# One change to an attention and feed-forward kernel: the score maxima from half of TensorE's rows, two query tiles at a time

## The reference

```python
y = x * jax.lax.rsqrt(jnp.mean(x * x, axis=-1, keepdims=True) + RMS_EPS) * rms_w
y = jnp.einsum('bsm,cm->bsc', y, w_in)
...
q = _rope(q)
k = _rope(k)
qk = jnp.einsum('bghsd,bgxpd->bghsp', q, k) * DQK ** (-0.5)
causal = jnp.tril(jnp.ones((s, s), dtype=bool))
qk = jnp.where(causal, qk, -jnp.inf)
attn = jax.nn.softmax(qk, axis=-1)
o = jnp.einsum('bghsp,bgxpd->bghsd', attn, v)
```

## Time and profile before

| | |
|---|---|
| median of the runs shown | 1998.78 us (1995.89 to 2000.47) |
| the profiled execution's own time | 2001.82 us |
| its span, first to last instruction | 2000.0 us |
| PE busy in the span | 1920.8 us (96%) |
| POOL busy in the span | 1423.1 us (71%) |
| attention stage, first to last of POOL's low parts | 71 to 1462 us |
| mean granted clock of TensorE | 0.983 of full speed |

### The profile page before, as it was taken

The page is one execution under the profiler, slowest core; times in us unless marked ns, Lnnn a source line. Parts: engine busy times, 40 slices in busy tenths (PEclk is TensorE's granted clock), DMA queues, the critical chain, the costliest instruction groups (busy, mean ns, idle before and its releaser), DMA issues. The chain is left out here.

```text
span 2000.0 us, 55133 instructions
## 1 busy us (share of the span) xinstructions
PE 1920.8 (96%) x21382; PEld 1184.5 (59%) x21382; DVE 1233.8 (62%) x3283; ACT 936.9 (47%) x1969; POOL 1423.1 (71%) x1627
## 2 busy tenths in 40 slices
PE   4999979999999999999999999999969998999999
PEld 3566656666666666666666666666634443444444
DVE  7787568668768776876887687687625562221221
ACT  4465546556655565665556566555622211111110
POOL 1799979999999999999999999999920001121211
PEclk7999989999999999999999999999989999999999
DMA  6342262244225224321522442152156520000000
GB/s 209 67 78 39 67 147 49 44 65 74 46 41 105 49 44 70 73 45 39 105 49 44 76 70 48 33 94 47 37 183 217 209 85 1 16 5 21 5 16 22
DMA packets 301572, 136.79 MB, mean 68 GB/s; under 512 B 248336, under 2 KB 285456, under 8 KB 299792
## 3 DMA queue, kind: packets, MB, share of 16 engines
q1 hardware_dynamic: 301328, 133.43, 29.6%
HBM read 49.48 MB, written 25.17 MB: 37 GB/s over the span
## 5 line engine op out<-in xcount | busy, mean ns | idle before, releaser
L786 POOL TENSOR_TENSOR pl<-p 128x512 f16<-128x512 f32 (+3 forms) x1280 | 1137.4, 919 | 38.6 <-ACT p L635 35.3
L635 ACT ACTIVATE p<-a_ps 128x512 f32<-128x512 f32 (+3 forms) x1280 | 677.5, 532 | 570.9 <-PE a_ps L568 333.9
L701 DVE TENSOR_REDUCE mpart<-a_ps 128x1 f32<-128x512 f32 x768 | 508.6, 685 | 140.6 <-PE a_ps L552 136.0
L584 PE MATMUL a_ps<-v,p 128*128 128x65 f16 x4352 | 528.1, 193 | 6.2 <-POOL pl L786 5.6
L586 PE MATMUL a_ps<-v,p 128*128 128x64 f16 x4352 | 530.6, 194 | 0.0
L588 PE MATMUL a_ps<-v,pl 128*128 128x65 f16 x4352 | 527.4, 192 | 0.0
L584 PEld LDWEIGHTS a_ps<-v,p 128*128 128x128 bf16 x4352 | 412.7, 97 | 110.1 <-issue 7.9
L586 PEld LDWEIGHTS a_ps<-v,p 128*128 128x128 bf16 x4352 | 406.1, 97 | 108.3 <-issue 0.3
L552 PE MATMUL a_ps<-k_hl,q_hh 128*128 128x512 f16 (+3 forms) x1280 | 429.7, 348 | 17.0 <-issue 15.7
L568 PE MATMUL a_ps<-q_lm,k_h 128*128 128x512 f16 (+3 forms) x1280 | 444.6, 347 | 0.0
L567 PE MATMUL a_ps<-q_hh,k_hl 128*128 128x512 f16 (+3 forms) x1280 | 443.7, 347 | 0.0
(11 more groups left out here) (95 smaller groups left out, 2268.6 us busy)
## 6 DMA issues: line engine op xcount, KB each, us to landing
attn_scratch<-o_turn SPq DMA_DIRECT2D x64, 256.0 KB, 3.0
p_att<-attn_scratch SPq DMA_DIRECT2D x32, 512.0 KB, 4.3
raw<-ffn_t SPq DMA_DIRECT2D x12, 1024.0 KB, 5.0
wraw<-w_in_t SPq DMA_DIRECT2D x8, 768.0 KB, 5.3
resid_scratch<-raw SPq DMA_DIRECT2D x4, 1024.0 KB, 4.4
raw<-w_out_t SPq DMA_DIRECT2D x1, 4096.0 KB, 15.9
x<-resid_scratch SPq DMA_DIRECT2D x4, 1024.0 KB, 8.0
out<-x SPq DMA_DIRECT2D x16, 256.0 KB, 2.1
```

Source lines behind the costliest of these rows:

```text
L584: nc.tensor.matmul(o, weights, v[:, par, j, 0:VU], start=(j == 0 and t == 0), stop=False, skip_group_check=True)
L635: nc.scalar.activation(p32[:, i % RING, r * P:CHUNK], sbank(i)[:, r * P:CHUNK], ACT.Exp, scale=SCALE).then_inc(exp_done, 1)
L701: nc.vector.reduce_max(mpart[:, u % 2, t, kk:kk + 1], bank, AX.X).then_inc(maxs_used, 1)
L786: nc.gpsimd.tensor_tensor(pl[:, i % RING, cols], p32[:, i % RING, cols], p_high[:, i % RING, cols], ALU.subtract).then_inc(low_ready, 1)
```

## The change

The product for the maxima uses k's high part alone, which is 64 rows deep. Two of them run as a pair: the first takes rows 0 to 63 of `q_hh` and of `k_h1`, the second rows 64 to 127 of `q_hh` and of `k_hl`, which both hold the high parts. The pair is two query tiles against the same chunk of keys, each into its own bank; both banks are taken before the first product. `query_and_key_tile` puts the pieces in an order in which two that follow each other are such a pair. The order of the slots moves each second piece into the slot of the first. Nothing else is changed: the number and the widths of the products and of DVE's reductions are the same.

```diff
@@ -249,7 +249,7 @@
 def opening():
 
     out = [(None, ("proj", 0, t), []) for t in range(2 * TPC)] + [(None, None, [])] * 2
-    out += [(None, None, [(0, u, i)]) for u in range(HG) for i in range(KEY_TILES[u])]
+    out += [(None, None, [(0, u, i), (0, u, i + 1)]) for u in range(HG) for i in range(0, KEY_TILES[u], 2)]
     return out
...
         for i in range(KEY_TILES[u]):
-            pieces[begin + i * (end - begin) // KEY_TILES[u]].append((ahead, u, i))
+            pieces[begin + i // 2 * 2 * (end - begin) // KEY_TILES[u]].append((ahead, u, i))
...
-            for item in [("piece", *p) for p in pieces[:1]] + ([job] if job else []) + [("piece", *p) for p in pieces[1:]]]
+            for item in [("piece", *p) for p in pieces[:2]] + ([job] if job else []) + [("piece", *p) for p in pieces[2:]]]
+
+
+def query_and_key_tile(u, i):
+
+    pair, second = divmod(i, 2)
+    both, kk = divmod(pair, u // HG + 1)
+    return 2 * both + second, kk
...
-                def max_piece(ahead, u, i):
+                def max_pair(ahead, u, i):
                     c, h = divmod(u, HG)
-                    t, kk = divmod(i, c + 1)
                     if i == 0:
                         pe.wait_ge(hh_in[c % 2][h], 16 * (2 * (g + ahead) + c // 2 + 1))
                         if h == 0:
                             pe.wait_ge(k_in[c], 32 * (g + ahead + 1))
-                    bank = take_bank("piece", ahead, u, i)
-                    width = CHUNK if kk < c else (t + 1) * P
-                    nc.tensor.matmul(bank[:, 0:width], q_hh[:, c % 2, h, t * P:(t + 1) * P],
-                                     k_hl[:, par ^ ahead, kk * CHUNK:kk * CHUNK + width], start=True, stop=True)\
-                        .then_inc(maxs_ready, 1)
+                    banks = [take_bank("piece", ahead, u, n) for n in (i, i + 1)]
+                    for n, (rows, keys) in enumerate(((slice(0, DH), k_h1), (slice(DH, P), k_hl))):
+                        t, kk = query_and_key_tile(u, i + n)
+                        width = CHUNK if kk < c else (t + 1) * P
+                        nc.tensor.matmul(banks[n][:, 0:width], q_hh[rows, c % 2, h, t * P:(t + 1) * P],
+                                         keys[rows, par ^ ahead, kk * CHUNK:kk * CHUNK + width], start=True, stop=True)\
+                            .then_inc(maxs_ready, 1)
...
-                    for piece in pieces[:1]:
-                        max_piece(*piece)
+                    for piece in pieces[:2:2]:
+                        max_pair(*piece)
...
-                    for piece in pieces[1:]:
-                        max_piece(*piece)
+                    for piece in pieces[2::2]:
+                        max_pair(*piece)
...
                 def reduce_piece(ahead, u, i):
                     gg, (c, h), n = g + ahead, divmod(u, HG), FIRST_STEP[u] + i
-                    t, kk = divmod(i, c + 1)
+                    t, kk = query_and_key_tile(u, i)
...
-                    for piece in pieces[:1]:
+                    for piece in pieces[:2]:
                         reduce_piece(*piece)
...
-                    for piece in pieces[1:]:
+                    for piece in pieces[2:]:
                         reduce_piece(*piece)
```

## The result

The changed kernel takes 2036.2 us (median; 2035.1 to 2037.4) against 1999.6 us for the kernel before (1995.9 to 2001.5): a ratio of 1.0186, with an interval of 1.0168 to 1.0203. That is 36.6 us slower, where 1949 us, 51 us faster than that median, was forecast. The profiled execution took 2035.3 us, 33.5 us more than the one of before.

A forecast was written before the change was run, and what follows sets the result against it. PE and POOL were both taken as full, with POOL becoming the bound and capping the gain at 62 us. Taking 50 from the profiled 2001.8 us gave 1952, less 3.0 for the median: 1949 us; 8-in-10 range 1934 to 2110.

The forecast's parts named there:

- Removed from PE: Products for the maxima: pairs cost only their wider product, saving PE 13.8 us in each group of four heads.
- Added on PE: Changes to half height and back around each pair: two bare weight loads, 60 ns a pair, 4.8 us a group.
- rival A: Before and behind every pair the array runs empty: 390 ns a pair, 2138 us; chance 0.24 in full.
- the price for half of the tail: Half the overlapping tail bare at height changes: 225 ns a pair, +34 us, 2033 us; in-between switches' chance 0.23.
- ACT, POOL and SP issue the same instructions and transfers in the same order: Queues of these three engines: claimed unchanged by the change, with no cost counted.
- Waits and order on PE: Two banks taken at once, products a slot earlier, DVE's reductions reordered: priced at nothing while POOL is the bound.
- the cover: PE's spare time in a group once POOL is the bound, 2.3 us, taken to hide waits and order.
- Rival C: Pairs wait for DVE to free banks in crowded stretches: 26 us back on PE, 1975 us; chance 0.07.
- POOL as the bound: Attention groups: PE falls to 164.1 us, under POOL's 166.4, so POOL limits and PE waits for its low parts.
- Of the 62 us I take 50: POOL's usable idle time over all groups caps the gain at 62 us; 50 taken, about a fifth staying idle.
- Rival B: A pair's halves run one behind the other, so PE streams as before plus switching: 1999 to 2250 us; chance 0.06.
- the signs for A: 100 ns or more ahead of each pair and again behind it, and POOL's idle time grows.

The follow-up runs named there:

- e5: The changed kernel with SP's transfers put back in the order of the kernel before: 2024.8 us, ratio 1.0128.
- e6: The changed kernel with all pairs at full height and SP's transfers in the order of before: 2007.0 us, ratio 1.0032.
- e2: The changed kernel with both half-height products of a pair on the same rows, so they run one behind the other: 2144.3 us, ratio 1.0724.
- e8: The kernel before, in its own order, with every product for the maxima singly at half height: 2241.9 us, ratio 1.1215.
- e9: The changed kernel with SP's order of before, off-diagonal products as two half-height pairs in a row, diagonal ones singly at full height: 2008.6 us, ratio 1.0038.

## Why the prediction was wrong

The loss of 36.6 us in three parts, each from a pair of kernels that differ in it alone: **17.9 us** from halving less its changes of height (e5 against e6), **11.4 us** from SP's order (the change against e5), **7.2 us** from the pairs' own order (e6 against before). Taken one behind the other they must add up to the loss, but the first two were each measured twice: halving is 17.4 us with SP's order moved, and SP's order 11.9 us at full height.

- *Removed from PE, 13.8 us a group:* right. Taking the overlap away costs 108 us of the 110 (e2), and the steps of 215 ns hold within one height.
- *Added on PE, 60 ns a pair:* **this step failed, by its size.** It measured 200 ns in the trace (96 + 104), 204 in e8, and (17.9 + 110) / 625 = 205 between e5 and e6. The number of changes was nearly right: 625, or 78 a group, where the text has 80, as 15 pairs stand right behind another. The reason given, that the change from products to transposes loses nothing, came from a row that has no change of height: both of those are 128 rows high. The bare weight load of the earlier trace rows, 30 ns between load and product, was not what was paid either: at a change the load starts 4 or 5 ns ahead of its product. Of its own bounds, 0 and 390 ns, the price lies in the middle, above the 172 ns that the text named as the point from which rival A decides. With 200 ns the prediction's own formula gives 173.1 - 13.8 + 80 x 0.200 = 175.3 us a group, 2.2 us more, 18 us in all. So rival A's place is what was seen, and over half of the 165 ns that it charges for the tail on each side (96 and 104 ns). That the price for half of the tail came to 2033 us, 3 us from the result, is luck: it put 34 us on the switches, where 17.9 were measured, and the rest came from the order. That the array runs empty at a change was an estimate, and no run shows it: the trace shows both loads of a change late by some 0.1 us, each way (91 to 100 ns).
- *"ACT, POOL and SP issue the same instructions and transfers in the same order":* **false for SP,** and it cost 11.4 us. The diff shows the cause: it changes the slots from which SP's times are computed. The prediction read the order on PE and DVE alone.
- *Waits and order on PE, priced at nothing "while POOL is the bound":* the cover never came, and the order cost 7.2 us. Rival C's mechanism, waits of the pair for DVE, is small in the change (4.2 us for the reductions L709). At full height and with SP's order of before (e6), POOL's low parts wait 44.7 us for ACT, where it was 35.3. That scores come later behind two products than behind one fits this. By starts on PE, e6's attention stage loses 3.4 us more than before ahead of the products for the maxima, 2.5 ahead of the scores and 1.2 ahead of the values; what brings each about was not tested.
- *POOL as the bound, "Of the 62 us I take 50":* never reached, since PE got slower. That ceiling was not tested by any run.
- *Rival B:* refuted by starts 3 ns apart and by e2.
- *What would show it:* the signs for A were the ones seen, 100 ns ahead of the pair and again behind it, and POOL's idle time grown. "A median over 2003 us says that the halving is worth less than its switches" held, but the median alone would have charged all 36.6 us to it, and half belongs to the order.

## What to carry to other kernels

Halving the height of a product pays here only for what stays together: a change of height there and back cost some 200 ns, about the time of one 512-column product (215 ns), so a single pair between full-height work gains nothing and a narrow one loses. Two pairs behind one change gained 17 us of the 44 that were due; about half of the rest went to waits for the banks of their results. The order that puts two pairs side by side cost 26 us by itself, so a change like this pays only where the order costs less. When slots are moved by a formula, compare the order on every queue that computes its times from them, SP's among them.

## What the runs showed of the hardware

- A half-height pair is as fast as one product of its width, its two products 3 ns apart, and pairs follow each other almost without loss (0.23 us where 512 columns take 0.215, e9) when no bank is waited for. A load for the other height starts only 4 or 5 ns ahead of its product (604 of 616 changes to half height, all 615 back), 0.1 us late, both on the way in and on the way out, where between full-height products the load starts with the product ahead (within 5 ns in 16152 of 16834).
- Some short waits cost more than their length here. In the changed kernel the granted clock fell from 1.00 to 0.50 behind three of the seven group starts other than the one where the DMA engines are full (share 1.05, 329 GB/s from 251 to 267 us): where the step into the first pair was 2.6, 2.2 and 2.3 us. Where it was 1.8, 1.5 and 1.4 us, and in the last group, without such a step, the clock stayed. In all seven PE also stood idle for 0.60 us ahead of one pair. In e5 one step of 1.5 us was followed by such a fall, and in the kernel before one of 2.05 us was not, so the length of the wait alone does not decide it. In the stretch from 986.40 to 989.80 work took about twice its usual steps (408 and 427 ns for 512 columns where it is 215, 107 for 128 where it is 56), so each fall, 3.4 us at half, costs some 1.7 us on top of the wait, by estimate. In the attention stage the clock stood at half for 23.9 us in the changed kernel's trace and for 13.7 us in e5's; half of the difference, some 5 of SP's 11.4 us, is an estimate of the clock's part in it.
